# Four stage borders of a graph-and-experts kernel: earlier first gathers, slots written elsewhere, another order of first groups

## The reference

```python
# layer 0: attention over edges, on x_norm = layernorm(layernorm(x))
q, k, v = x_norm @ Wq + bq, x_norm @ Wk + bk, x_norm @ Wv + bv      # 8 heads of 64
ws  = einsum("ehd,ehd->eh", q[src], k[dst]) * SCALE * edge_attr_8
e   = exp(ws - segment_max(ws, src)[src]); att = e / segment_sum(e, src)[src]
val = segment_sum(att * v[dst], src)
x   = x + layernorm(x) + (val @ W1 + b1) @ W2 + b2
# layer 0: 16 experts in 4 groups, 2 groups and 2 experts of each chosen by softmax, top-p 0.9
xf  = layernorm(x); tw = routing(xf)
x   = x + sum_e tw[:, e] * ((silu(xf @ W1[e]) * (xf @ W3[e])) @ W2[e])
# layer 1: two graph convolutions, then (h + x) / 2
conv(x) = relu(diag * (x @ W0) + segment_sum(edge_w * (x @ W1)[src], dst) + b)
x   = x + (conv(conv(layernorm(x))) + layernorm(x)) * 0.5
# layer 1: 8 experts, top 2 of the router's logits, a layernorm in each expert
xf  = layernorm(x); gates = softmax(top2(xf @ router_w))
x   = x + sum_e w_e * layernorm_e(xf + relu(xf @ w1[e] + b1[e]) @ w2[e] + b2[e])
```

## Time and profile before

| | us |
|---|---|
| median of 3 runs | 2596.5 (2593.6 to 2597.51) |
| profiled execution, own time | 2598.54 |
| its span | 2596.4 |
| mean granted TensorE clock | 0.956 of full |

### The profile page before, as it was taken

The page is one execution under the profiler, slowest core; times in us unless marked ns, Lnnn a source line. Parts: engine busy times, 40 slices in busy tenths (PEclk is TensorE's granted clock), DMA queues, the critical chain, the costliest instruction groups (busy, mean ns, idle before and its releaser), DMA issues. The chain is left out here.

```text
span 2596.4 us, 33633 instructions
## 1 busy us (share of the span) xinstructions
PE 2363.2 (91%) x10815; PEld 1862.8 (72%) x10818; DVE 1763.5 (68%) x4161; ACT 1133.5 (44%) x2077; POOL 690.7 (27%) x644
## 2 busy tenths in 40 slices
PE   6799885999999999999588999999986799999998
PEld 4577664777777777777466878888865577777776
DVE  7677696777777777776455665555554577777775
ACT  6554322435444444535342222222234766666651
POOL 5455413121121211110131222222222433333310
PEclk9899987999999999999799999999988899999999
DMA  4211133121221212120342343433346556666631
GB/s 153 58 50 50 18 118 114 37 94 63 84 85 62 98 50 98 53 90 33 119 162 97 129 143 129 132 129 131 125 145 181 103 145 163 147 151 160 144 99 47
DMA packets 156034, 271.90 MB, mean 105 GB/s; under 512 B 35442, under 2 KB 36082, under 8 KB 155638
## 3 DMA queue, kind: packets, MB, share of 16 engines
q1 hardware_dynamic: 122918, 203.00, 23.7%
q0 software_dynamic: 32976, 67.19, 11.3%
HBM read 185.82 MB, written 100.41 MB: 110 GB/s over the span
## 5 line engine op out<-in xcount | busy, mean ns | idle before, releaser
L1284 POOL TENSOR_TENSOR d_rs<-d_ve,net_half_neg 128x4 f32<-128x4 f32 x58 | 68.3, 1178 | 509.6 <-DVE d_ve L1330 422.8
L2221 ACT ACTIVATE conv_h<-conv_h 128x512 f32<-128x512 f32 x79 | 50.0, 632 | 308.1 <-DVE conv_h L2173 265.1
L2668 POOL DMA_INDIRECT next_own<-message,d_at x79 | 127.1, 1609 | 164.7 <-DMA next_own<-own 142.7
L2143 DVE TENSOR_TENSOR conv_yl<-conv_pty,conv_yh 128x512 fp32r<-128x512 f32 x79 | 54.7, 692 | 151.5 <-ACT conv_yh L2217 141.4
L1290 POOL DMA_INDIRECT d_val<-values,net_slot_s x79 | 84.6, 1071 | 189.1 <-DVE d_x L1407 87.8
L1601 ACT ACTIVATE d_act_out<-d_pa 128x512 f32<-128x512 f32 (+1 forms) x80 | 46.0, 575 | 200.6 <-PE d_pa L70 200.6
L68 PE MATMUL conv_p<-conv_w_hi,conv_yh 128*128 128x512 f32 x316 | 132.5, 419 | 0.6 <-DVE conv_yl L2143 0.6
L68 PE MATMUL d_po<-shared_wq_hi,d_hh 128*128 128x512 f32 x316 | 129.0, 408 | 1.2 <-DVE d_hl L1413 0.3
L68 PE MATMUL d_pc<-d_xh,shared_wv_hi 128*128 128x512 f32 (+1 forms) x320 | 129.6, 405 | 0.0
L68 PE MATMUL d_pa<-d_xh,shared_wk_hi 128*128 128x512 f32 (+1 forms) x320 | 129.1, 403 | 0.0
L68 PE MATMUL conv_p<-conv_w_hi,conv_hh 128*128 128x512 f32 x316 | 124.4, 394 | 2.1 <-DVE conv_hl L2143 2.1
(11 more groups left out here) (565 smaller groups left out, 7189.5 us busy)
## 6 DMA issues: line engine op xcount, KB each, us to landing
y<-d_y SPq DMA_DIRECT2D x79, 256.0 KB, 2.0
conv_yin<-y SPq DMA_DIRECT2D x79, 256.0 KB
h<-conv_h SPq DMA_DIRECT2D x79, 256.0 KB, 2.0
own<-conv_own SPq DMA_DIRECT2D x79, 256.0 KB
next_own<-own SPq DMA_DIRECT2D x79, 256.0 KB, 4.7
next_x<-y SPq DMA_DIRECT2D x79, 256.0 KB, 2.7
out<-d_res SPq DMA_DIRECT2D x79, 256.0 KB, 2.7
early_x<-in_x SPq DMA_DIRECT2D x10, 1024.0 KB
```

What stands on the lines that cost most here:

```text
L1284: pool.tensor_tensor(rs[n][:], ve[n][:], k.half_neg[:, 0:T], ALU.pow).then_inc(pow_done[n], 1)
L2143: v.tensor_tensor(lo[:, t % 2, :], bank[t % 2][:], hi[:, t % 2, :].bitcast(F32), ALU.subtract)\
L2221: act_.activation(h[:, t, :], h[:, t, :], ACT.Relu).then_inc(h_made, 1)
L2668: pool.indirect_dma_start(own[n][:, t, :], None, k.message2[:, :], bass.IndirectOffsetOnAxis(ap=at[:, t:t + 1], axis=0), bounds_check=EP + ...
```

## The change

It touches four borders between stages.

1. Sorting to q/k/v: the buffers and semaphores of gathered rows move to the outer holder; the four gathers of group 0's source rows are issued by GpSimd at the end of `sort_sources`, after a wait for the sorted records. To make room, `w12` there takes the place of a used weight stage, with two more waits on ScalarE. In `project_edges` GpSimd does two gathers of destinations, the sources' powers, the other two gathers, the destinations' powers; VectorE takes the sources' statistics first and puts its memsets and copies between the rounds, and takes the destinations' statistics after the sources' low halves.
2. The 20 scatters of the destinations' slots and their load leave `project_edges`; in `dense0_phase` each of the first ten bodies of GpSimd issues two of them, and SyncE loads the table before its last body.
3. Aggregation to experts: the buffer `val` moves to `Early`; group 0's four gathers of values are issued at the end of GpSimd's list in `aggregate_values`, after the stores they read from. In `dense0_phase` the adds of group 0 alternate with its statistics, and `out` of the aggregation takes the softmax's buffer.
4. The last stage: no copy to `at`; a message semaphore for each of the two buffers, so that a group's gathers don't wait for those of the group before; the hand-written beginnings of ScalarE, VectorE and TensorE in another order; group 0's four transposes go to four banks (`turn_bank`) and don't wait for low halves.

```diff
@@ attention_phase, sort_sources
+            r.rows = {x: cr.sb(f"rows_{x}", [P, T, D]) for x in "sd"}
+            r.rows_in = {x: [cr.sem(f"rows_in_{x}{t}") for t in range(T)] for x in "sd"}
+def gather_rows(pool, a, k, r, x, g, t):
+    n = "sd".index(x)
+    pool.indirect_dma_start(r.rows[x][:, t, :], None, a["x"][:, :],
+                            bass.IndirectOffsetOnAxis(ap=k.rec["s"][:, T * g + t, n:n + 1], axis=0),
+                            bounds_check=NPAD - 1, oob_is_err=False).then_inc(r.rows_in[x][t], 16)
-        w12 = c.sb("w12", [P, KC, D])
+        w12 = stage[0]
...
+            pool.wait_ge(sorted_in, 16)
+            for t in range(T):
+                gather_rows(pool, a, k, r, "s", 0, t)
...
+            act_.wait_ge(split_done, KC)
+            act_.wait_ge(bias_done, 1)
@@ project_edges
-        load_slots("d")
-        sp.wait_ge(slots_in, 32)
+        sp.wait_ge(slots_in, 16)
...
-        for x in "sd":
-            gather(0, x)
-        for x in "sd":
-            powers(0, x)
+        for t in range(2):
+            gather_rows(pool, a, k, r, "d", 0, t)
+        powers(0, "s")
+        for t in range(2, T):
+            gather_rows(pool, a, k, r, "d", 0, t)
+        powers(0, "d")
...
-        scatter_slots("d", range(ET))
...
+        s = statistics(v, 0, "s")
         for t in (headsel4[:], attr4[:], repeat):
             v.memset(t, 0.0).then_inc(zeroed, 1)
         for t in spreads:
             v.memset(t[:].bitcast(F32), 0.0).then_inc(zeroed, 1)
+        statistics2(v, 0, "s", s)
...
+        statistics3(v, 0, "s", s)
...
-        s = statistics(v, 0, "s")
-        statistics2(v, 0, "s", s)
-        statistics3(v, 0, "s", s)
+        for t in range(T):
+            split_lo(v, 0, "s", t)
         s = statistics(v, 0, "d")
-        split_lo(v, 0, "s", 0)
-        split_lo(v, 0, "s", 1)
         statistics2(v, 0, "d", s)
-        split_lo(v, 0, "s", 2)
         statistics3(v, 0, "d", s)
-        split_lo(v, 0, "s", 3)
@@ aggregate_values
-    out = c.sb("out", [P, 2, D])
+    out = soft.expo
...
+        for n in range(2):
+            pool.wait_ge(stored[n], 16 + 16 * ET // 2)
+        pool.wait_ge(empty_rows, 16)
+        for t in range(T):
+            gather_values(pool, k, early, 0, t)
@@ dense0_phase
+            sp.wait_ge(slots_out, 16 * ET)
+            sp.dma_start(k.slot["d"][:], k.slots["d"].rearrange("(p n) o -> p (n o)", p=P)).then_inc(slots_in, 16)
             body(0, NG)
+            sp.wait_ge(slots_in, 16)
...
+                if g < ET // 2:
+                    for t in range(2 * g, 2 * g + 2):
+                        pool.indirect_dma_start(k.slots["d"][:, :], bass.IndirectOffsetOnAxis(ap=k.slot_at[:, t:t + 1], axis=0),
+                                                own_place[:, t:t + 1], None, bounds_check=NPAD - 1,
+                                                oob_is_err=False).then_inc(slots_out, 16)
...
-            for g in range(2):
-                for t in range(T):
-                    gather(g, t)
+            for t in range(T):
+                gather(1, t)
             power(0, 1)
...
+            add(0, 0, 0)
             for t in range(T):
-                add(0, 0, t)
-            front1_begin(0, 0)
-            front1(0, 0)
+                if t < T - 1:
+                    add(0, 0, t + 1)
+                v.wait_ge(x1_made, 4 + t + 1)
+                if t < T - 1:
+                    v.bn_stats(st[1][:, t, :], x[0][:, t, :])
+            statistics(v, 0, 0, 1, T - 1)
@@ dense1_phase
+        def turn_bank(g, t):
+            return (ptr, pq[0], pq[1], px)[t] if g == 0 else ptr
...
-                if later(i, c_):
-                    for t in range(T):
-                        pool.wait_ge(msg_in[t], 16 * g)
-                hold(pool)
-                pool.tensor_copy(at[:], k.slot["d"][:, ds(T * g, T)]).then_inc(at_made, 1)
-                pool.wait_ge(at_made, g + 1)
...
-                                            bass.IndirectOffsetOnAxis(ap=at[:, t:t + 1], axis=0),
-                                            bounds_check=EP + P - 1, compute_op=ALU.add).then_inc(msg_in[t], 16)
+                                            bass.IndirectOffsetOnAxis(ap=k.slot["d"][:, T * g + t:T * g + t + 1], axis=0),
+                                            bounds_check=EP + P - 1, compute_op=ALU.add).then_inc(msg_in[n][t], 16)
...
+            for n in range(2):
+                for t in range(T):
+                    scale_y(0, n, t)
             for t in range(T):
                 half(0, 0, t)
-                scale_y(0, 0, t)
             for t in range(T):
                 square(0, 0, t)
+            norm(0, 0, 0)
+            for t in range(1, T):
+                norm(0, 0, t)
+                high(0, 0, t - 1)
+            high(0, 0, T - 1)
             for t in range(T):
                 half(0, 1, t)
-            for t in range(T):
-                norm(0, 0, t)
-            for t in range(T):
-                scale_y(0, 1, t)
-                high(0, 0, t)
+            small_copy(0)
             for t in range(T):
                 square(0, 1, t)
-            small_copy(0)
...
             gains_of(0, 0)
+            gains_of(0, 1)
             mean_of(0, 0)
             for t in range(T):
                 sum_(0, 0, t)
+            gains_of(0, 2)
             variance_of(0, 0)
-            gains_of(0, 1)
             shifts(0, 0)
+            for t in range(T):
+                low(0, 0, t)
             mean_of(0, 1)
             for t in range(T):
                 sum_(0, 1, t)
-                low(0, 0, t)
+            logits_of(0, 0)
             variance_of(0, 1)
-            gains_of(0, 2)
             shifts(0, 1)
-            logits_of(0, 0)
...
-                if t or not (isinstance(g, int) and g == 0):
+                if g:
                     pe.wait_ge(xl_made, 4 * g + t)
...
                 if main:
                     up(g, n, 0)
+                if g == 0:
+                    turn_small(0)
                 if mid:
                     turn(g + 1, 0)
...
             logits(0, 0, True)
-            turn_small(0)
```

More of the change, by code:

```diff
@@ L301, in __init__ @@
         self.x_in = [c.sem(f"x_in{n}") for n in range(2)]
+        self.val, self.val_in = c.sb("val", [P, T, D]), [c.sem(f"val_in{t}") for t in range(T)]
         self.weight_in, self.weight_high, self.weight_low = (
@@ L533, in project_edges @@
     same, rec = k.same, k.rec
-    rows = {x: c.sb(f"rows_{x}", [P, T, D]) for x in "sd"}
+    rows, rows_in = r.rows, r.rows_in
     st = {x: c.sb(f"st_{x}", [P, T, 6]) for x in "sd"}
@@ L556, in project_edges @@
     p_score, p_attr = c.ps("p_score"), c.ps("p_attr")
-    rows_in = {x: [c.sem(f"rows_in_{x}{t}") for t in range(T)] for x in "sd"}
     stats = {x: c.sem(f"stats_{x}") for x in "sd"}
@@ L584, in next_keys @@
                   .then_inc(keys_in, 16)
-        def load_slots(x):
-            sp.wait_ge(slots_out[x], 16 * ET)
-            sp.dma_start(k.slot[x][:], k.slots[x].rearrange("(p n) o -> p (n o)", p=P)).then_inc(slots_in, 16)
         next_keys("s", k.rec_s, 0)
-        load_slots("s")
+        sp.wait_ge(slots_out, 16 * ET)
+        sp.dma_start(k.slot["s"][:], k.slots["s"].rearrange("(p n) o -> p (n o)", p=P)).then_inc(slots_in, 16)
         sp.wait_ge(r.scattered, 16 * ET)
@@ L991, in _, with gather_values @@
                 project(pe, "d", "wv", cc).then_inc(v_done, 1)
+def gather_values(pool, k, early, g, t):
+    pool.indirect_dma_start(early.val[:, t, :], None, k.values[:, :],
+                            bass.IndirectOffsetOnAxis(ap=k.slot["s"][:, T * g + t:T * g + t + 1], axis=0),
+                            bounds_check=EP + P - 1, oob_is_err=False).then_inc(early.val_in[t], 16)
 def aggregate_values(nc, a, k, stack, hi, lo, early, soft, spreads, value):
@@ L1170, in dense0_phase @@
         x = early.x + [c.sb(f"x{n}", [P, T, D]) for n in range(2, XS)]
-        val = c.sb("val", [P, T, D])
+        val, val_in = early.val, early.val_in
         xf = c.sb("xf", [P, T, D])
@@ L1207, in dense0_phase @@
         x_in = early.x_in + [c.sem(f"x_in{n}") for n in range(2, XS)]
-        val_in = [c.sem(f"val_in{n}") for n in range(T)]
         y_out = [c.sem(f"y_out{n}") for n in range(2)]
@@ L1288, in gather @@
                 pool.wait_ge(x1_made, 4 * g + t + 1)
-                hold(pool)
-                pool.indirect_dma_start(val[:, t, :], None, k.values[:, :],
-                                        bass.IndirectOffsetOnAxis(ap=k.slot["s"][:, T * g + t:T * g + t + 1], axis=0),
-                                        bounds_check=EP + P - 1, oob_is_err=False).then_inc(val_in[t], 16)
+                gather_values(pool, k, early, g, t)
             def body(i, c_):
@@ L2592, in dense1_phase @@
         y_in, own_in = k.y_in, k.own_in
-        msg_in, out_done = ([c.sem(f"{n}{t}") for t in range(T)] for n in ("msg_in", "out_done"))
```

(4 more changed lines are left out.)

45 lines of the change are left out of this document (23 added, 22 removed).

## The result

| | before | after |
|---|---|---|
| median of 8 runs of each, us | 2594.49 (2591.26 to 2597.51) | 2586.43 (2581.63 to 2589.12) |
| ratio | 1 | 0.9971 (95%: 0.9962 to 0.9980) |
| profiled execution, own time | 2598.54 | 2586.63 |
| its span, mean granted clock | 2596.4, 0.956 | 2584.6, 0.958 |

The change gains 8.1 us between the medians, 0.29% by the ratio. I had forecast 20.5 (2574 from 2594.5) or, against the time of my profile, 22.8. The direction was right, the size was not.

What follows compares the result with a forecast made beforehand. TensorE, busy 91% of the span, was taken as the bound, leaving 233 us idle. Terms -1.2, -8.7, 0, -2.7 and -10.2 sum to -22.8, giving 2573.7 us from a 2596.5 median; range 2568 to 2590.

Steps and rivals of the forecast that it cites:

- GpSimd is busy from 58.2 to 63.2, the barrier waits for it: Sorting to q/k/v: four early gathers, issued 1.30 apart, hold the barrier only for their issue, costing every engine 5.1 us.
- DVE starts at 65.05 rather than 59.88: Start of q/k/v: VectorE's first instruction comes 5.1 us later, behind the early gathers; the border still gains 1.2 us net.
- the normalize 1.8 earlier: Q/k/v stage: ScalarE's normalize of source rows starts at 72.45 instead of 74.28, as the power begins sooner.
- My upper end of +2: Sorting to q/k/v: worst end of the range, a 2 us loss if the held barrier costs 5.1 and only 3.1 returns.
- DVE's first instruction 4.9 later: Start of expert stage: VectorE begins at 420.2 instead of 415.28 behind four early gathers; the border still gains 2.7 us.
- -8.7 if the stall goes: End of q/k/v: ScalarE's 10.09 us idle near 320 was blamed on the 20 scatters; moving them saves 8.7 us.
- rival A: End of q/k/v: the stall stays, moves or was only in the profile; total gain 14.1, time 2582.4 us; chance 0.34.
- Nothing of this stage waits for it [GpSimd]: End of q/k/v: GpSimd is not late; the slots' load lands some 13 us before the block ends at 333.6.
- Border 4, -10.2: Start of last stage: group 1's first transpose 12.0 us earlier, less 1.8 for half clock after a PE hole: 10.2 gained.
- Scatters in the expert stage, 0: Expert stage: two scatters, 2.6 us, in each of ten groups cost nothing, as the gathers finish 13.39 us before the power.
- rival D: Expert stage: GpSimd's slack is gone, so each of ten groups pays 2.6 us for its scatters; time 2608; chance 0.05.
- Rival C: All borders pay half: engines held at barriers, landings delayed, clock low longer, stall stays; time 2589 us; chance 0.10.

## Why the prediction was right or wrong

- **Borders 1 and 3, the same step: "GpSimd is busy from 58.2 to 63.2, the barrier waits for it".** I priced the early gathers at their issue and took it that the border is over when GpSimd has issued them. It is over when they have landed. That puts 3.0 us more on each border, and together they make the largest part of the error: by the runs they lose 6.5 and 4.3 where I had gains of 1.2 and 2.7, 14.7 in all (10.4 by the traces), against 8.7 at border 2.
- **Border 1, "DVE starts at 65.05 rather than 59.88" and "the normalize 1.8 earlier": wrong by 4.1.** 1.1 because I read the end of VectorE's list as the landing of the records, and 3.0 net for the wait: 3.8 from the last gather's end to the drain's end, less 0.8, as VectorE follows GpSimd's drain by 1.03 and not by the 1.85 that I read from its own idle time. -1.2 became +5.1 in the traces (half clock behind the longer hole included), 6.5 in the runs. My upper end of +2 assumed a held barrier but not a longer one. The chain behind that start was right to 0.1, except for the twelve q matmuls.
- **Border 3, "DVE's first instruction 4.9 later": wrong by 3.1 for the same reason.** It was 8.0. -2.7 became +1.4 in a level pair of traces. The other part, 0.7 for the power behind group 1's gathers, I had missed as well.
- **Border 2, "-8.7 if the stall goes": wrong, the largest single term.** The stall was in the one profiled execution: the runs show 0 for this border, twice, within 4 to 5 us. The step that failed is the check against the runs. I took 2.04 of excess over a median of three as a sign that a stall of 8.7 was in those runs too. By eight runs the excess was 4.05, and the profile without the stall lies 4.9 under the median of the runs taken beside it (2593.76): executions of this kernel differ by more than I allowed. That no row named a cause I had said, and given the case 0.34; with it (rival A) I would still have been too low, at 2582. "Nothing of this stage waits for it [GpSimd]" was wrong as well: it held only under the stall, and without it GpSimd's drain held the block by 2.0 to 2.3 us in three profiles. So in this part of the change a small gain is there, by the very wait that I had overlooked at borders 1 and 3. As to what made the stall: not found. The back-pressure of the block that writes records (the Trainium skill, "NOTIFIC — the notification-queue block", section 7.1) would fit an event that comes and goes, but no run here shows it.
- **Border 4, -10.2: right in place and order, and in size by luck:** two errors cancel, group 0's rows 1.6 later (1.2 of it at the first gather, as dropping the copy brought 0.3 and not 1.06) and no clock lost in the hole that I had charged 1.8 for. The runs give 13.6 and 15.6, more than the traces (9.4 and 11.1). One trace of the old order kept the low clock for longer, at 3.6 us; that this is the rest of the difference is not shown.
- **Scatters in the expert stage, 0: right as far as the power goes,** idle 10.77 as reckoned; rival D did not happen.
- **Rival C** (2589, engines held at the barriers) came nearest in the number and had the right place, at a price too small; I had given it 0.10. Its "group 1's landings delay group 0's" is not shown.
- **The reading of the slices was wrong,** though no term hangs on it. PE does not dip to 8 where the stages meet, but to 5 at 389 to 454 and at 1233 to 1298, and to 6 and 7 at 1947 to 2077. The dip at the end of the expert stage, as deep as that of border 3, none of the four parts aims at.

The sum by the runs: +6.5 (1), 0 (2), +4.3 (3), -13.6 (4), together -3 with an uncertainty of some 8; measured -8.1.

## What to carry to other kernels

A DMA that GpSimd issues at the end of a block is not "in flight over the border". In every trace here the block ended only after it had landed, so it hides its issue and its latency behind nothing and holds all engines for both. Before work is moved to the end of a list, look at the drain of that engine, and for the end of a block at the row of the engine that ended last, not at the idle time of another. Before a stall with no named cause is made a term of a sum, it needs a second profile: a single trace can hold 10 us that no other execution has, and the clock behind a restart of PE differed by 3.6 us of time between two traces of the same code. Of a change that touches several borders each should be timed alone; here one of four carried nearly all the gain, and alone it beat the whole (0.9940 against 0.9971).

## What the runs showed of the hardware

- GpSimd's drain at the end of a block did not end before the transfers on its queue had landed: 0.1 to 0.2 us behind the last gather's landing at border 3, 1.0 at border 1. From the end of the last gather to VectorE's next instruction it was 4.2 to 4.9 us, and no longer with 2.04 us of work in between; with no gather open it was 2.03 from GpSimd's last instruction (border 3, before).
- After 20 scatters the drain ended 6.8 to 7.1 us behind the last landing, in the three profiles without the stall. What it waits for is open.
- Two executions of one kernel can differ by 9.7 us of span (2596.4 and 2586.7) at nearly the same mean granted clock (0.956 and 0.958).
- In a PE hole of 2.75 us the granted clock fell to half, at about 462.4; in one of 2.63 us it did not, and stayed full behind it; in one of 4.05 us it stayed full too, and fell 1.2 us after PE had begun again (90.8).
- In the last stage, with the same code and starts 0.99 us apart, the full clock came back 3.2 us behind the first logits in one execution (2035.93) and 12.2 behind in the other (2045.96).
